# A state space and expert kernel: the front taken by pairs of batches, D as a diagonal matmul, deviations on GpSimd

## The chip, the cores and the metric

One core of a Trainium2 chip. The metric is the device time of one execution in microseconds (us), as the median of several runs. PE is TensorE, DVE VectorE, ACT ScalarE, POOL GpSimd; SP issues most DMAs.

## What is computed

For u of 16 batches x 512 positions x 256 features:

```python
xn = layernorm(u)
Bu = einsum('bld,nd->bln', xn, B_w)              # 64 states
h  = causal convolution over l with sigmoid(log_lambda) ** t, per state
y  = einsum('bln,dn->bld', h, C_w) + D * xn
aff = (xn @ waff.T) / (|xn| * |waff|)            # 8 experts
# best expert of each row, kept if its rank in its batch and expert is below a capacity
# that comes from the mean of all aff and the threshold
out = u + y + sum over experts of (gelu(xn * mask @ W1 + b1) @ W2 + b2)
```

A row that an expert does not get still adds gelu(b1) @ W2 + b2 of that expert (the "zero rows" of the code).

## The kernel before

**Front.** A batch is 512 positions, held as 128 partitions of 4 quarters of 256 features (`QD` = 1024 columns). For each of 16 batches:

- DVE takes `bn_stats` of each quarter (`moments`, L926), aggregates them for two batches (`variance`, L933, L935); ACT takes the root (`deviation`, L519), DVE makes 1/deviation with one Newton step and -mean/deviation (`rstd_of`, L943 to L947).
- ACT normalises the four quarters (`normal`, L525). PE transposes them (`turn`, L675) into `ps_t`, ACT copies that to `xnt` (`turned`, L533), two buffers.
- PE multiplies by 64 columns of B and 8 of waff at once (`states_in`, L693, 72 output rows), DVE runs the recurrence on all 72 rows with one scan instruction (`states`, L953; the factor is 0 for the 8 router rows). PE transposes the 8 rows back (`routed`, L699) and multiplies the states by C (`states_out`, L707) into `ps_y`. DVE adds `ps_y` to the row base (`add_y`, L959).
- POOL makes `D * xn` (L394) and adds it to u (L398), four quarters each; this is the base to which y is added.

Beside this, 12 of the 16 weight units (W1 and W2 of 8 experts) are split into a high and a low f16 part: ACT sums the absolute values (`weight_sum`, L538), PE brings the sum to all partitions (`bound`, L721), DVE makes a power of two of it (`weight_scales`, L963 to L967), ACT makes the high part (`high_part`, L544), DVE the low part (`low_part`, L982). Which batch has which of these steps is written in the tables `SUMS` and `HIGHS`. SP's queue brings in u and the weights and stores xn and base to DRAM. Raw weights lie in a ring of four, and the split parts take the places of xn and base of earlier batches (`home_free`).

**Passage.** From the numerators of all batches (`ps_num`) DVE makes the affinities (L1092) and the best expert; PE transposes them (L761); DVE finds the capacity and the keys (from L1103), counts (L1128 to L1137 behind PE's L780, L781) and places; ACT searches the thresholds (L598 to L600). PE also makes the zero rows (`zero_row`, L750). POOL then gathers the rows of each tile by indirect DMAs.

**Tiles.** 39 tiles of 256 rows go through W1 (L836 to L838), Gelu on ACT, a split on DVE, W2 (L860 to L862), DVE's last operations, and an indirect store. This part is not changed.

Each engine runs its instructions in the order in which they are written; all waits are semaphores written by hand. What a PE instruction waits for also holds all that stands behind it.

## Time and profile before

| | us |
|---|---|
| median of 3 runs | 648.92 (647.56 to 649.32) |
| the profiled execution | 647.61 |
| its span | 645.9 |
| PE busy in the span | 586.8 (91%) |
| DVE busy | 500.3 (77%) |
| POOL busy | 460.1 (71%) |
| ACT busy | 339.8 (53%) |
| mean granted clock of TensorE, share of full speed | 0.951 |

The page of the profile gives busy time per engine, groups of instructions by line, and the chain of work that ended last. Busy time of PE counts overlapping records once. A wait that the trace ascribes to an engine is one that this engine ended last.

### The profile page before, as it was taken

The page shows a single profiled execution, that of the slowest core. Times are in us where ns is not written, and L with a number is a line of the kernel's source. Part 1 is how long each engine was busy: PE and PEld are TensorE (multiplying, and loading weights), DVE is VectorE, ACT ScalarE, POOL GpSimd, SP SyncE. Part 2 cuts the span into 40 slices and gives each one's busy share as a digit, 9 for nine tenths or more (in the row PEclk, how much of TensorE's full clock was granted, in tenths as well). Part 3 has the DMA queues.
Part 4 walks back from the last instruction along what each step waited for, and adds up shares of the span by engine and source line. Part 5 has one row for each costly group of instructions (what it writes and reads, how often), then busy time and mean ns, then how long its engine had stood idle before and what let it go on. Part 6 is the DMA issues. An engine that isn't in the chain of part 4 may idle for free.

```text
span 645.9 us, 15995 instructions
## 1 busy us (share of the span) xinstructions
PE 586.8 (91%) x4597; PEld 496.1 (77%) x4598; DVE 500.3 (77%) x971; ACT 339.8 (53%) x637; POOL 460.1 (71%) x629
## 2 busy tenths in 40 slices
PE   2988878898679989978999999999999999999994
PEld 1655555666567879867898989898998989898983
DVE  5789989798999699669778676767676777767673
ACT  4877859755867926534535353535353444444440
POOL 1999987940068626888788888887778777878463
PEclk9988869897897999989999999999999999999998
DMA  8994776628310214342212222222112112211100
GB/s 312 411 371 150 247 254 186 225 110 261 130 43 17 60 30 155 130 132 59 83 58 81 64 66 81 64 71 73 55 47 70 57 44 73 73 45 29 49 30 2
DMA packets 33587, 72.63 MB, mean 112 GB/s; under 512 B 6519, under 2 KB 19088, under 8 KB 33552
## 3 DMA queue, kind: packets, MB, share of 16 engines
q1 hardware_dynamic: 21488, 46.67, 20.5%
q0 software_dynamic: 11232, 25.20, 12.8%
q10 hardware_dynamic: 832, 0.31, 0.2%
q8 instruction: 19, 0.31, 0.2%
q14 instruction: 16, 0.13, 0.1%
HBM read 50.64 MB, written 27.00 MB: 120 GB/s over the span
## 4 chain that ended last, share of the span: by engine, by line
PE 61%; DVE 19%; issue 8%; ACT 6%; POOL 4%; DMA 1%; DVEq 0%; ACTq 0%; POOLq 0%; SPq 0%
PE ps_bu L860 9%; PE ps_bu L861 9%; PE ps_bu L862 9%; PE ps_t L836 4%; PE ps_t L838 4%; PE ps_t L837 4%; PE ps_y L837 4%; PE ps_y L838 4%; PE ps_y L836 4%; ACT area L525 2%; PE ps_y L707 2%; PE ps_bu L693 2%; PE ps_t L675 2%; POOL out L452 2%; DVE wsum L991 1%
## 5 line engine op out<-in xcount | busy, mean ns | idle before, releaser
L860 PE MATMUL ps_bu<-area,ring 128*128 x624 | 170.1, 273 | 1.9 <-issue 1.8
L861 PE MATMUL ps_bu<-area,ring 128*128 x624 | 170.1, 273 | 0.0
L862 PE MATMUL ps_bu<-area,ring 128*128 x624 | 170.1, 273 | 0.0
L1295 DVE SCALAR_TENSOR_TENSOR ring<-ring,h_scale 128x512 f16<-128x512 f32 x156 | 117.8, 755 | 5.5
L638 ACT ACTIVATE ring<-ps_t,b1t,inv_in 128x256 f32<-128x256 f32 x156 | 79.4, 561 | 56.4 <-PE ps_t L838 46.0
L452 POOL DMA_INDIRECT out<-ring,idx_b x78 | 93.0, 1193 | 18.3 <-issue 13.4
L437 POOL DMA_INDIRECT work<-xn_rows,idx_x x78 | 86.7, 1112 | 26.2 <-issue 21.1
L462 POOL DMA_INDIRECT work<-base_rows,idx_b x78 | 90.9, 1165 | 18.0 <-issue 15.2
L1304 DVE SCALAR_TENSOR_TENSOR ring<-ps_bu,inv_out,work 128x256 f32<-128x256 f32 x78 | 34.1, 479 | 77.5 <-PE ps_bu L862 75.8
L638 ACT ACTIVATE ring<-ps_y,b1t,inv_in 128x256 f32<-128x256 f32 x156 | 79.4, 562 | 21.7 <-PE ps_y L838 21.1
L836 PE MATMUL ps_t<-work,area 128*128 128x256 f16 x312 | 87.0, 279 | 2.4 <-issue 2.2
L838 PE MATMUL ps_t<-work,area 128*128 128x256 f16 x312 | 87.0, 279 | 0.0
L837 PE MATMUL ps_t<-work,area 128*128 128x256 f16 x312 | 87.0, 279 | 0.0
L385 POOL TENSOR_TENSOR small<-ones 128x1 f32<-128x1 f32 x156 | 46.4, 297 | 55.6 <-DVE ring L1319 23.7
L836 PE MATMUL ps_y<-work,area 128*128 128x256 f16 x312 | 85.2, 273 | 0.0
L837 PE MATMUL ps_y<-work,area 128*128 128x256 f16 x312 | 85.2, 273 | 0.0
L838 PE MATMUL ps_y<-work,area 128*128 128x256 f16 x312 | 85.2, 273 | 0.0
L1292 DVE TENSOR_SCALAR ring<-ring,h_scale 128x512 f16<-128x512 f32 x156 | 79.3, 509 | 2.1 <-issue 0.3
L394 POOL TENSOR_TENSOR work<-area,d_bc 128x256 f32<-128x256 f32 x64 | 59.2, 957 | 20.9 <-DMA thr_bc<-L_ffn_affinity_threshold 12.0
L860 PEld LDWEIGHTS ps_bu<-area,ring 128*128 128x128 f16 x624 | 61.0, 98 | 9.4 <-issue 2.4
L861 PEld LDWEIGHTS ps_bu<-area,ring 128*128 128x128 f16 x624 | 61.0, 98 | 7.2
L862 PEld LDWEIGHTS ps_bu<-area,ring 128*128 128x128 f16 x624 | 61.0, 98 | 7.0
(272 smaller groups left out, 1075.4 us busy)
## 6 DMA issues: line engine op xcount, KB each, us to landing
ring<-L_ffn_W SPq DMA_DIRECT2D x14, 1024.0 KB, 6.5
xn_rows<-area SPq DMA_DIRECT2D x8, 1024.0 KB, 8.7
base_rows<-area SPq DMA_DIRECT2D x8, 1024.0 KB, 6.9
area<-L_attn_u SPq DMA_DIRECT2D x7, 1024.0 KB, 18.5
work<-L_ffn_W SPq DMA_DIRECT2D x4, 1024.0 KB, 6.1
area<-L_ffn_W SPq DMA_DIRECT2D x2, 1024.0 KB, 6.3
work<-xn_rows,idx_x POOLq DMA_INDIRECT x78, 2.8
work<-base_rows,idx_b POOLq DMA_INDIRECT x78
```

The source lines that it names most:

```text
L437: g.indirect_dma_start(out=xg[r % 2][:, h * D:(h + 1) * D], out_offset=None, in_=xn_dram, in_offset=bass.IndirectOffsetOnAxis(ap=idx_x[:, ...
L452: g.indirect_dma_start(out=out_rows, out_offset=bass.IndirectOffsetOnAxis(ap=idx_b[:, 2 * ro + h:2 * ro + h + 1], axis=0), in_=og[ro % 2][ ...
L462: g.indirect_dma_start(out=bg[rb % 2][:, h * D:(h + 1) * D], out_offset=None, in_=base_dram, in_offset=bass.IndirectOffsetOnAxis(ap=idx_b[ ...
L638: ins = a.activation(h32[:, c * W:(c + 1) * W], ps_h[qt][:, c % CQ * W:(c % CQ + 1) * W], ACT.Gelu, bias=b1t[:, bass.ds(e * C + c, 1)], sc ...
L836: t.matmul(dst, wh, xhi[p][:, k, :], start=(k == 0), stop=False)
L837: t.matmul(dst, wh, xlo[p][:, k, :], start=False, stop=False)
L838: last = t.matmul(dst, wl, xhi[p][:, k, :], start=False, stop=(k == K - 1))
L860: t.matmul(dst, hh, wh, start=(c == 0), stop=False)
L861: t.matmul(dst, hh, wl, start=False, stop=False)
L862: last = t.matmul(dst, hl, wh, start=False, stop=(c == C - 1))
L1292: v.tensor_scalar(hhi[p][:, cs], h32[:, cs], h_scale[:, bass.ds(e, 1)], None, ALU.mult).then_inc(s["f_hhi"], 1)
L1295: v.scalar_tensor_tensor(out=hlo[p][:, cs], in0=h32[:, cs], scalar=h_scale[:, bass.ds(e, 1)], in1=hhi[p][:, cs], op0=ALU.mult, op1=ALU.sub ...
```

## The change

- Batches are taken by pairs. `states_in` writes the 64 states of the first batch to partitions 0 to 63 and those of the second to 64 to 127; one scan serves both. C and lambda are loaded twice, for both halves.
- `routed` no longer transposes rows of the scan. It multiplies the transposed xn by the 8 columns of waff, 16 matmuls per pair, and needs no scan.
- D * xn is no longer made on POOL. PE multiplies transposed xn by the diagonal of D (two 128x128 blocks) and accumulates onto C's product, in two halves `states_out(i, 0)` and `(i, 1)` per pair; `add_y` comes in two halves too and adds to u itself. `xnt` has four buffers.
- The aggregation, the root and Newton's steps go from DVE and ACT to POOL (`deviations`: 19 operations on 128x8 per pair, with a power of -0.5 and two Newton steps).
- ACT normalises three quarters of a batch, POOL the fourth.
- Sums, bounds, scales, high and low parts come in pairs. The last two of the 12 high parts stand behind the affinities. The places of xn and base in `area` are changed, and so is the order of SP's queue.
- At the end `routed` of the last pair stands ahead of its states; the zero rows 0 and 1 stand behind the transposes of the affinities.

```diff
-        d_bc = sb("d_bc", D)
+        diag = sb("diag", K * P)
+        diag_k = diag[:, :].rearrange("p (k d) -> p k d", k=K)
...
+        xnt = [part(work, at, QD).rearrange("p (k s) -> p k s", k=K) for at in (3 * QD, 4 * QD + E * D + TE, 0, QD)]
...
             def xn_store(i):
                 sp.wait_ge(s["xn_ok"], 2 * i + 2)
+                sp.wait_ge(s["xq_ok"], 2 * i + 2)
...
+            for i in range(1, 5):
+
+                base_store(i)
+                xn_store(i + 3)
+                raw_in(2 * i + 2)
+                raw_in(2 * i + 3)
...
-            pool.wait_ge(s["p_late"], 4 * 16)
-            for b in range(B):
-
...
+            minus_half = cnt[:, 6:7]
+            g.memset(minus_half, -0.5)
+
+            def deviations(i):
+
+                c = slice(2 * i * Q, (2 * i + 2) * Q)
+                st = stats[:, 12 * i * Q:12 * (i + 1) * Q].rearrange("p (t m) -> p t m", m=6)
+                r_, v_, n_, d_, m_ = rstd[:, c], ve[:, c], newt[:, c], sq_d[:, c], sum_d[:, c]
+                pool.wait_ge(s["st_ok"], i + 1)
+                g.tensor_tensor(mean2[:, c], st[:, :, 1], st[:, :, 4], ALU.add)
+                g.tensor_tensor(m_, st[:, :, 2], st[:, :, 5], ALU.add)
+                link(g.tensor_tensor(d_, st[:, :, 1], st[:, :, 4], ALU.subtract))
+                g.tensor_scalar(m_, m_, 1.0 / D, None, ALU.mult)
+                link(g.tensor_tensor(d_, d_, d_, ALU.mult))
+                link(g.tensor_scalar(d_, d_, 0.25, None, ALU.mult))
+                link(g.tensor_tensor(var[:, c], m_, d_, ALU.add))
+                link(g.tensor_scalar(v_, var[:, c], EPS, None, ALU.add))
+                link(g.tensor_tensor(r_, v_, minus_half.to_broadcast([P, 2 * Q]), ALU.pow))
+                for _ in range(2):
+                    link(g.tensor_tensor(n_, r_, r_, ALU.mult))
+                    link(g.tensor_tensor(n_, n_, v_, ALU.mult))
+                    link(g.tensor_scalar(n_, n_, -0.5, 1.5, ALU.mult, ALU.add))
+                    link(g.tensor_tensor(r_, n_, r_, ALU.mult))
+                link(g.tensor_tensor(n_, mean2[:, c], r_, ALU.mult))
+                g.tensor_scalar(nmr[:, c], n_, -0.5, None, ALU.mult).then_inc(s["rstd_ok"], 1)
+                pool.wait_ge(s["rstd_ok"], i + 1)
+
+            for i in range(PAIRS):
+                deviations(i)
+                for b in (2 * i, 2 * i + 1):
+
+                    for q in (3,):
+                        t, cols = b * Q + q, slice(q * D, (q + 1) * D)
+                        last = g.tensor_scalar(xn_(b)[:, cols], xu_(b)[:, cols], rstd[:, t:t + 1], nmr[:, t:t + 1],
+                                               ALU.mult, ALU.add)
+                    last.then_inc(s["xq_ok"], 1)
...
             def normal(b):
                 act.wait_ge(s["rstd_ok"], b // 2 + 1)
-                for q in range(Q):
+                for q in range(3):
...
             def turned(b):
+
+                wait(act, s["y_ok"], b // 2 * 2 - 2)
+                wait(act, s["num_ok"], b // 2 - 1)
                 for k in range(K):
                     act.wait_ge(s["xt_ok"], K * b + k + 1)
-                    wait(act, s["bu_ok"], b - 1)
-                    a.copy(xnt[b % 2][:, k, :], ps_t[:, k * S:(k + 1) * S]).then_inc(s["xt_out"], 1)
+                    a.copy(xnt[b % 4][:, k, :], ps_t[:, k * S:(k + 1) * S]).then_inc(s["xt_out"], 1)
...
-            deviation(0)
             normal(0)
             normal(1)
             turned(0)
-            act.wait_ge(s["p_early"], 4 * 16)
-            a.activation(lam[0:N, 1:2], lam[0:N, 0:1], ACT.Exp, scale=-1.0).then_inc(s["lam_exp"], 1)
-            for b in range(B):
-
-                if b % 2 == 0 and b // 2 + 1 < PAIRS:
-                    deviation(b // 2 + 1)
-                if b + 1 < B:
-                    turned(b + 1)
-                if b + 2 < B:
-                    normal(b + 2)
-                if b == 1:
+            act.wait_ge(s["p_early"], 6 * 16)
+            a.activation(lam[:, 1:2], lam[:, 0:1], ACT.Exp, scale=-1.0).then_inc(s["lam_exp"], 1)
+            turned(1)
+            normal(2)
+            normal(3)
+            for i in range(PAIRS - 1):
+
+                if i + 2 < PAIRS:
+                    normal(2 * i + 4)
+                    normal(2 * i + 5)
+                if i >= 2:
+                    for n in (2 * i - 4, 2 * i - 3):
+                        high_part(n, raw_at(n))
...
+                turned(2 * i + 2)
+                turned(2 * i + 3)
+                if i == 0:
                     act.wait_ge(s["b1_ok"], 1)
                     a.activation(small[:, 0:E], ps_g[:, 0:E], ACT.Sqrt).then_inc(s["act_const"], 1)
                     a.activation(gelu_b[:, :], b1t[:, :], ACT.Gelu).then_inc(s["gelu_ok"], 1)
-                if b == 13:
-                    act.wait_ge(s["xnorm_ok"], 1)
-                    a.activation(sq0, xnorm, ACT.Sqrt).then_inc(s["xroot_ok"], 1)
-                if b in HIGHS:
-                    high_part(HIGHS.index(b), raw_at(HIGHS.index(b)))
-                if b in SUMS:
-                    weight_sum(SUMS.index(b))
+                else:
+                    weight_sum(2 * i - 2)
+                    weight_sum(2 * i - 1)
...
+            for n in (EARLY - 2, EARLY - 1):
+                high_part(n, raw_at(n))
...
-            def states_in(b):
-                pe.wait_ge(s["xt_out"], K * (b + 1))
-                wait(pe, s["scan_ok"], b - 1)
+            turn(1)
+
+            def states_in(i):
+
+                pe.wait_ge(s["xt_out"], K * (2 * i + 2))
+                wait(pe, s["scan_ok"], i - 1)
                 for k in range(K):
-                    last = t.matmul(ps_bu[b % 2][0:NE, :], bwk[:, k, :], xnt[b % 2][:, k, :], start=(k == 0), stop=(k == K - 1))
+                    for h in range(2):
+                        last = t.matmul(ps_bu[i % 2][h * N:(h + 1) * N, :], bwk[:, k, 0:N], xnt[(2 * i + h) % 4][:, k, :],
+                                        start=(k == 0), stop=(k == K - 1))
                 last.then_inc(s["bu_ok"], 1)
 
-            def routed(b):
-                pe.wait_ge(s["scan_ok"], b + 1)
-                for q in range(Q):
-                    last = t.transpose(ps_num[:, q * P + b * E:q * P + (b + 1) * E], every_q(hs[b % 2][N:NE, :], q),
-                                       ident[N:NE, N:NE])
+            def routed(i):
+
+                pe.wait_ge(s["xt_out"], K * (2 * i + 2))
+                for b in (2 * i, 2 * i + 1):
+                    for q in range(Q):
+                        for k in range(K):
+                            last = t.matmul(ps_num[:, q * P + b * E:q * P + (b + 1) * E], every_q(xnt[b % 4][:, k, :], q),
+                                            bwk[:, k, N:NE], start=(k == 0), stop=(k == K - 1))
                 last.then_inc(s["num_ok"], 1)
 
-            def states_out(b):
-                pe.wait_ge(s["scan_ok"], b + 1)
-                wait(pe, s["base_ok"], b)
-                for q in range(Q):
-                    last = t.matmul(ps_y[:, q * D:(q + 1) * D], every_q(hs[b % 2][0:N, :], q), ct[0:N, :],
-                                    start=True, stop=True)
+            def states_out(i, r):
+
+                pe.wait_ge(s["scan_ok"], i + 1)
+                pe.wait_ge(s["diag_ok"], 1)
+                wait(pe, s["base_ok"], 2 * i + r)
+                for n in range(2):
+                    q = 2 * r + n
+                    for h in range(2):
+                        t.matmul(ps_y[:, h * 2 * D + n * D:h * 2 * D + (n + 1) * D], every_q(hs[i % 2][h * N:(h + 1) * N, :], q),
+                                 ct[h * N:(h + 1) * N, :], start=True, stop=False)
+                    for h in range(2):
+                        for k in range(K):
+                            at = h * 2 * D + n * D + k * P
+                            last = t.matmul(ps_y[:, at:at + P], every_q(xnt[(2 * i + h) % 4][:, k, :], q), diag_k[:, k, :],
+                                            start=False, stop=(k == K - 1))
                 last.then_inc(s["y_ok"], 1)
...
-            for b in range(B):
-                if b + 1 < B:
-                    turn(b + 1)
-                states_in(b)
-                if b == 0:
+            for i in range(PAIRS - 1):
+                if i > 0:
+                    states_out(i - 1, 0)
+                states_in(i)
+                if i == 0:
                     constants()
-                if b > 0:
-                    routed(b - 1)
-                    if b < B - 1:
-                        states_out(b - 1)
-                if b - 1 in SUMS:
-                    n = SUMS.index(b - 1)
-                    pe.wait_ge(s["wsum_ok"], n + 1)
+                else:
+                    states_out(i - 1, 1)
+                turn(2 * i + 2)
+                routed(i)
+                turn(2 * i + 3)
+                if i > 0:
+
+                    pe.wait_ge(s["wsum_ok"], 2 * i)
                     pe.wait_ge(s["dve_const"], 2)
-                    wait(pe, s["wscale_ok"], n)
-                    bound(n, ps_g[:, 0:P]).then_inc(s["bound_ok"], 1)
+                    wait(pe, s["wscale_ok"], i - 1)
+                    for n in range(2):
+                        last = bound(2 * i - 2 + n, ps_g[:, n * P:(n + 1) * P])
+                    last.then_inc(s["bound_ok"], 1)
+            routed(PAIRS - 1)
+            states_out(PAIRS - 2, 0)
+            states_in(PAIRS - 1)
+            states_out(PAIRS - 2, 1)
...
-            zero_row(0)
-            zero_row(1)
-            routed(B - 1)
...
-            states_out(B - 2)
+            zero_row(0)
+            states_out(PAIRS - 1, 0)
+            zero_row(1)
             zero_row(2)
...
+            def states(i):
+                dve.wait_ge(s["bu_ok"], i + 1)
+                wait(dve, s["y_ok"], 2 * i - 2)
+                v.tensor_tensor_scan(hs[i % 2], lam_c.to_broadcast([P, S]), ps_bu[i % 2][:, :], 0.0,
                                      ALU.mult, ALU.add).then_inc(s["scan_ok"], 1)
 
-            def add_y(b):
-                dve.wait_ge(s["y_ok"], b + 1)
-                dve.wait_ge(s["dx_ok"], 2 * b + 2)
-                v.tensor_tensor(xu_(b), ps_y[:, :], xu_(b), ALU.add).then_inc(s["base_ok"], 1)
+            def add_y(i, r):
+
+                dve.wait_ge(s["y_ok"], 2 * i + r + 1)
+                for h in range(2):
+                    x = xu_(2 * i + h)[:, r * 2 * D:(r + 1) * 2 * D]
+                    last = v.tensor_tensor(x, ps_y[:, h * 2 * D:(h + 1) * 2 * D], x, ALU.add)
+                last.then_inc(s["base_ok"], 1)
...
+            for i in range(PAIRS - 1):
+                if i > 0:
+                    add_y(i - 1, 0)
+                if i >= 2:
+                    weight_scales(i - 2)
+                states(i)
+                if i > 0:
+                    add_y(i - 1, 1)
+                if i == 0:
+                    setup()
+                if i + 3 < PAIRS:
+                    moments(2 * i + 6)
+                    moments(2 * i + 7)
+                if i == 0:
+                    w_norms()
...
+                if i >= 2:
+                    for n in (2 * i - 4, 2 * i - 3):
+                        low_part(n, raw_at(n))
...
+            add_y(PAIRS - 2, 0)
+            states(PAIRS - 1)
+            add_y(PAIRS - 2, 1)
+            weight_scales(UNIT_PAIRS - 1)
```

Order of PE in a pass of the loop. Before, from one batch to the next (L675 turn, L693 states, L699 router's transposes, L707 output by C, L721 bound):

```order
L675 MATMUL ps_t<-ident,area 128x128 x8
L693 MATMUL ps_bu<-work,bwt 72x512 x2
L699 MATMUL ps_num<-ident,work 128x8 x4
L707 MATMUL ps_y<-ct,work 128x256 x4
L721 MATMUL ps_g<-ident,wsum 128x128
L675 MATMUL ps_t<-ident,area 128x128 x8
L693 MATMUL ps_bu<-work,bwt 72x512 x2
L699 MATMUL ps_num<-ident,work 128x8 x4
L707 MATMUL ps_y<-ct,work 128x256 x4
```

With the change, one pass, from the second half of states_out(i-1, 0) on (L742 is C, L747 is D, L720 states, L699 turn, L730 the router's numerators, L761 the two bounds):

```order
L742 MATMUL ps_y<-ct,work 128x256 x2
L747 MATMUL ps_y<-diag,work 128x128 x4
L720 MATMUL ps_bu<-work,bwt 64x512 x4
L742 MATMUL ps_y<-ct,work 128x256 x2
L747 MATMUL ps_y<-diag,work 128x128 x4
L742 MATMUL ps_y<-ct,work 128x256 x2
L747 MATMUL ps_y<-diag,work 128x128 x4
L699 MATMUL ps_t<-ident,area 128x128 x8
L730 MATMUL ps_num<-bwt,work 128x8 x16
L699 MATMUL ps_t<-ident,area 128x128 x8
L761 MATMUL ps_g<-ident,wsum 128x128 x2
```

The bound stood behind the states and the output of the next batch; the two bounds now stand directly behind the second turn of the pass.

Order of ACT in the same place, before (L538 weight sum, L519 root, L533 copies of the turned batch, L525 normal, L544 high part):

```order
L538 ACTIVATE work,wsum<-ring 128x2048
L519 ACTIVATE rstd<-work 128x8
L533 COPY work<-ps_t 128x512 x2
L525 ACTIVATE area<-area,work,rstd 128x256 x4
L544 ACTIVATE area<-ring,scale_w 128x2048
L538 ACTIVATE work,wsum<-ring 128x2048
```

With the change, one pass and the start of the next (L541 normal, L562 high parts, L551 copies, L556 weight sums):

```order
L541 ACTIVATE area<-area,work,rstd 128x256 x6
L562 ACTIVATE area<-ring,scale_w 128x2048 x2
L551 COPY work<-ps_t 128x512 x4
L556 ACTIVATE work,wsum<-ring 128x2048 x2
L541 ACTIVATE area<-area,work,rstd 128x256 x6
```

The sums for which the two bounds wait are made behind the copies of both batches that PE turned last before those bounds.

Order of PE at the end of the front, before (L750 zero rows, L761 transposes of the affinities, L780 and L781 the counts):

```order
L699 MATMUL ps_num<-ident,work 128x8 x4
L721 MATMUL ps_g<-ident,wsum 128x128
L750 MATMUL ps_t<-ring,gelu_b 128x256 x16
L699 MATMUL ps_num<-ident,work 128x8 x4
L761 MATMUL ps_t<-ident,work 128x128 x4
L764 MATMUL ps_num<-small,ones 128x1
L707 MATMUL ps_y<-ct,work 128x256 x4
L750 MATMUL ps_g<-ring,gelu_b 128x256 x8
L780 MATMUL ps_bu<-rc,tri 128x8
L781 MATMUL ps_bu<-rc,ones 128x8
```

With the change, from the end of states_out(6, 1) to the counts (L806 transposes of the affinities, L798 zero rows, L827 and L828 the counts):

```order
L747 MATMUL ps_y<-diag,work 128x128 x4
L806 MATMUL ps_t<-ident,work 128x128 x4
L809 MATMUL ps_num<-small,ones 128x1
L798 MATMUL ps_t<-ring,gelu_b 128x256 x8
L742 MATMUL ps_y<-ct,work 128x256 x2
L747 MATMUL ps_y<-diag,work 128x128 x4
L742 MATMUL ps_y<-ct,work 128x256 x2
L747 MATMUL ps_y<-diag,work 128x128 x4
L798 MATMUL ps_t<-ring,gelu_b 128x256 x8
L798 MATMUL ps_g<-ring,gelu_b 128x256 x8
L827 MATMUL ps_bu<-rc,tri 128x8
L828 MATMUL ps_bu<-rc,ones 128x8
```

Zero rows 0 and 1 moved from ahead of the transposes of the affinities to behind them, and one more half output stands between these and the counts; ahead of these rows the last pair's states and both halves of the output of pair 6 come after the last numerators.

## Rows read from the trace of the kernel before

**Rows 1.** stretches: us, busy us (instructions) of each engine, PEclk, DMA share, GB/s

```profile
80.00:100.00 20.00, 16.66 (x51) 11.02 (x52) 17.97 (x39) 12.78 (x19) 17.82 (x21) 0.66 0.59 208
300.00:400.00 100.00, 100.00 (x919) 90.04 (x917) 76.27 (x138) 42.12 (x81) 81.91 (x123) 1.00 0.23 71
```

**Rows 2.** chain of waits, in order of time: start us, us, what

```profile
128.21 1.71 PE ps_t L675 x8
```

**Rows 3.** groups by line, first 170 us: count | busy us, mean ns | idle us before

```profile
L394 POOL TENSOR_TENSOR work<-area,d_bc 128x256 f32<-128x256 f32 x64 | 59.2, 957 | 20.9 <-DMA thr_bc<-L_ffn_affinity_threshold 12.0 <-ACT area L525 7.5
...
L707 PE MATMUL ps_y<-ct,work 64*128 64x256 f32 x128 | 41.1, 469 | 10.8 <-DVE area L959 10.8
...
L982 DVE SCALAR_TENSOR_TENSOR area<-ring,scale_w,area 128x2048 f16<-128x2048 f32 x10 | 24.6, 2461 | 0.1
...
L959 DVE TENSOR_TENSOR area<-ps_y,area 128x1024 f32<-128x1024 f32 x16 | 19.5, 1216 | 0.1
L953 DVE TENSOR_TENSOR_SCAN work<-lam,ps_bu 72x512 f32<-72x512 f32 x16 | 19.2, 1203 | 0.1
```

**Rows 4.** timeline of DVE: a small operation by itself and beside POOL's products

```profile
8.97 0.17 DVE L945 TENSOR_TENSOR work<-work 128x8 f32<-128x8 f32 x1
...
31.56 0.65 DVE L945 TENSOR_TENSOR work<-work 128x8 f32<-128x8 f32 x1
```

**Rows 5.** timeline: a small operation of POOL, the slow cast of DVE

```profile
2.19 0.22 POOL L371 CAST iota_f<-ring 128x40 f32<-128x40 int32 x1
...
178.23 2.14 DVE L1198 CAST tile_expert<-work 128x39 int32<-128x39 f32 x1
```

**Rows 6.** ACT: two copies (timeline), and a weight sum (chain of waits)

```profile
22.80 1.07 ACT L533 COPY work<-ps_t 128x512 f32<-128x512 f32 x2 [0.74 <-PE ps_t L675]
...
78.02 1.99 ACT work L538 x2
```

**Rows 7.** timeline of PE, 67 to 78 us

```profile
67.41 1.97 PE L675 MATMUL ps_t<-ident,area 128*128 128x128 f32 x8 [1.15 <-ACT area L525]
...
72.34 2.24 PE L707 MATMUL ps_y<-ct,work 64*128 64x256 f32 x8
74.51 0.49 PE L721 MATMUL ps_g<-ident,wsum 128*128 128x128 f32 x2
74.83 1.04 PE L675 MATMUL ps_t<-ident,area 128*128 128x128 f32 x8
75.71 1.88 PE L693 MATMUL ps_bu<-work,bwt 128*72 128x512 f32 x4
77.52 0.64 PE L699 MATMUL ps_num<-ident,work 8*128 8x8 f32 x4
```

**Rows 8.** timeline of PE's weight loads: three series of short passes

```profile
21.29 0.52 PEld L716 LDWEIGHTS ps_g<-ring,ones 128*128 128x128 f32 x4
...
169.04 0.63 PEld L773 LDWEIGHTS ps_num<-area 128*128 128x128 f16 x16 [4.79 <-DVE area L1186]
...
202.65 0.97 PEld L721 LDWEIGHTS ps_bu<-ident,wsum 128*128 128x128 f32 x8
```

**Rows 9.** timeline of the start, DVE, ACT and PE

```profile
4.42 2.88 DVE L926 BATCH_NORM_STATS2 work<-area 128x6 f32<-128x256 f32 x8 [4.29 <-DMA area<-L_attn_u]
...
9.57 4.04 ACT L525 ACTIVATE area<-area,work,rstd 128x256 f32<-128x256 f32 x8 [1.15 <-DVE work L947]
...
11.79 1.94 PE L675 MATMUL ps_t<-ident,area 128*128 128x128 f32 x8 [11.79 <-ACT area L525]
```

**Rows 10.** timeline of the end of the front

```profile
146.93 0.69 DVE L1092 TENSOR_TENSOR work<-ps_num,work 128x512 f32<-128x512 f32 x1 [0.73 <-PE ps_num L699]
...
150.55 0.69 DVE L1103 TENSOR_SCALAR_CACHE_REDUCE work<-work 128x512 f32<-128x512 f32 x1
...
159.36 0.16 DVE L1137 COPY end<-ps_bu 128x8 f32<-128x8 f32 x1
...
160.93 3.32 PEld L750 LDWEIGHTS ps_g<-ring,gelu_b 128*128 128x128 f32 x16 [0.23 <-issue]
```

More of the change, by code:

```diff
@@ L1016, in _ @@
             dve.wait_ge(s["consts"], 1)
-            link(v.tensor_scalar(lam[0:N, 2:3], lam[0:N, 1:2], 1.0, None, ALU.add))
-            link(v.reciprocal(lam[0:N, 3:4], lam[0:N, 2:3]))
+            link(v.tensor_scalar(lam[:, 2:3], lam[:, 1:2], 1.0, None, ALU.add))
+            link(v.reciprocal(lam[:, 3:4], lam[:, 2:3]))
+            moments(4)
+            moments(5)
             def setup():
@@ L1022, in setup @@
                 v.tensor_copy(c_bc[:, :], ps_g[:, 128:128 + D])
+                v.tensor_copy(d_col, ps_g[:, 384 + E * C:384 + E * C + K])
                 v.tensor_copy(b1t[:, :], ps_g[:, 384:384 + E * C]).then_inc(s["b1_ok"], 1)
+                dve.wait_ge(s["b1_ok"], 1)
+                for k in range(K):
+                    last = v.tensor_scalar(diag_k[:, k, :], ident[:], d_col[:, k:k + 1], None, ALU.mult)
+                last.then_inc(s["diag_ok"], 1)
                 dve.wait_ge(s["b1_ok"], 1)
@@ L1226, in kept @@
                 link(v.tensor_tensor(thr, bits[:, 3:4].bitcast(F32), sign, ALU.mult))
-                gt, run = gap, pick
+                gt = gap_kept
                 link(v.tensor_scalar(gt, a_rows, thr, 0.0, ALU.is_gt, ALU.add, accum_out=cnt[:, 3:4]))
```

215 lines of the change are left out of this document (73 added, 142 removed).

## Prediction

> **What bounds the kernel now.** I read, in this order, the table of stretches, the chain of waits, the groups by line of the first 170 us and the timelines of a few batches. The stretches [rows 1] divide the span in two: from 300 us on PE is busy without a break (100.00 of 100 us) at a granted clock of 1.00, while from 80 to 100 us no engine is quite full and the clock is 0.66. The change touches only the front (16 batches) and the passage from it to the expert tiles. A microsecond won or lost there moves everything behind it, since the tiles wait for the row indices that come out of it and then run on PE without slack. In these 20 us of the front DVE is busy 18.0, POOL 17.8, PE 16.7 and ACT 12.8 [rows 1]. The turns of batch 0 begin on PE at 11.79 [rows 9], those of batch 15 at 128.21 [rows 2]: 116.4 us for 15 batches, **15.5 us for a pair**. PE waits 10.8 us for DVE's add L959 before L707 alone [rows 3]. So DVE sets the pace now, with POOL close to it.
>
> **What DVE, ACT and POOL gain.** Per pair DVE loses eight L933, the addition L935 and the five small operations L943 to L947. One of these takes 0.17 us by itself and 0.65 beside POOL's long products [rows 4]; with the wait for ACT's root this is 2 to 5 us. One scan for two batches saves 1.2 us [rows 3]. What stays is 2.9 (statistics [rows 9]), 1.2 (scan), 2.4 (adds), two L982 of 2.46 [rows 3] and some 1 us of scales (five operations of 0.15 to 0.3): **12.4 us per pair**. POOL loses its 16 long operations (0.96 each for L394 [rows 3]) and gets two like them and 19 small ones. A small one takes 0.22 us with 0.06 to the next [rows 5], so 19 x 0.28 = 5.3 us, **7 us per pair** with the two quarters at 0.85. No row shows a power on POOL: 0.2 us is the floor, and the ceiling is 2.1, what a tiny cast took on DVE [rows 5]; I take 0.3, since POOL's other tiny operations lie there. ACT: six L525 of 0.5 (four of them per batch before [rows 9]), two high parts of 2.0, four copies of 0.53 and two sums of 2.0 [rows 6]: **13.1 us**. All three are below the 15.5 of now. By these engines alone the change would win.
>
> **What PE pays.** A matmul in f32 leaves two records, a transpose one: L716 is two matmuls, and x4 [rows 8]. I count passes (records) and take the distances between starts, not durations, which overlap. At full clock, per pair:
> - turns: 16 passes, as before. L675 begins at 74.83, the next line at 75.71 [rows 7]: 0.9 a batch, 1.8 a pair.
> - states: 8 passes of 512 columns, as before; 1.81 us per 4 (75.71 to 77.52 [rows 7]), 3.6 in line. They now alternate between two halves of the array's columns.
> - output by C: 16 passes; 2.17 us per 8 (72.34 to 74.51 [rows 7]), 4.3 in line. They now alternate between two halves of its rows.
> - new, D by the diagonal: 16 matmuls, 32 passes of 128 columns. Eight loads of that shape, L721, take 0.97 us, the last one 0.19 [rows 8]: a distance of 0.11. 32 x 0.11 = **3.5**.
> - new, the router's numerators by matmuls, in place of eight transposes of 1.1 us: 32 passes of 8 columns. L716 has exactly that shape: four loads in 0.52 us, the last 0.19 [rows 8], so 0.11 again although only 8 columns follow. **3.5**.
> - bounds: 4 passes, 0.5.
>
> The trace never has work in two halves side by side, so states and C are bounded by the line (3.6 and 4.3) and by half of it (1.8 and 2.15). I take the middle, 2.7 and 3.2: the two passes of one matmul use the same half, so only passes of neighbours can run together. The Trainium skill (TensorEngine Tiling (Array Packing), Key Properties) says that different tiles can execute weight loads and matmuls in parallel, and that a change of tiling mode drains the engine. By the first alone the pair would be 2.0 us shorter than I take it; no row of before shows either. The sum is 1.8 + 2.7 + 3.2 + 3.5 + 3.5 = **14.7 us** without bounds, against 1.8 + 3.6 + 4.3 + 1.1 = 10.8.
>
> **A new wait on PE.** The orders ahead of this text show it. In before a bound stands behind states and output of later batches, and ACT's sum is long done. Now two bounds stand right behind turn(2i+3), and ACT makes the two sums only after it has copied what that turn gives. PE's queue stops for the end of the copies (0.7 us: the second of two in 1.07 [rows 6]), 2 x 1.99 for the sums, and 0.1 for semaphores: **4.8 us** in every pass of the loop, i = 1 to 6. Queued behind it stand output, states and the next turns, and ACT's next copies and sums wait for these. It is a closed circle: turn, copies, sums, bounds, output, states, output, turn, numerators, turn. DVE (12.4) and ACT (13.1) fit inside.
>
> After idle time the granted clock falls from the level of 2.4 to that of 1.2 GHz: a turn costs 1.97 us after a gap of 1.15, and 1.04 otherwise [rows 7]. From 80 to 100 us the mean is 0.66 [rows 1], so 13.6 of 20 us are at the lower level, behind two gaps, 6.8 each. One gap per pass thus costs nothing at best (the low stretch falls in the gap) and 3.4 us at worst (all of it in work); I take the middle, 1.7. A pass is then 14.7 + 4.8 + 0.5 + 1.7 = **21.7 us**, against 15.5.
>
> **The start.** The first statistics end at 7.3 [rows 9]; POOL's deviations end at 12.6, 3 us behind the start of L525 now (9.57), and those of the next pairs at 19.6 and 26.6. ACT takes batches 4 and 5 ahead of the copies of batch 2: 26.6 + 3.1 = 29.7, copy 0.6, then PE's turn(3), 0.9. Pass i = 1 starts at some 31.5. A power of 2.1 us would come in three times, 5.4 us later.
>
> **The end of the front.** 31.5 + 6 x 21.7 = 161.7, numerators 3.5: the affinities start at 165.2, before at 146.93 [rows 10]: **+18.3**. Then PE has 3.35 + 2.7 + 3.35 = 9.4 us of output and states ahead of the transposes of the affinities, and DVE adds and scales until 11.8 us behind the affinities, where L1103 came at 3.6 [rows 10]. Next PE has 1.0 (transposes, sum), zero row 0 (3.4: sixteen L750 [rows 10]), an output (3.35) and zero rows 1 and 2 (6.8) before the counts: 9.4 + 1.0 + 3.4 + 3.35 + 6.8 + 0.4 = 24.4, against 159.36 - 146.93 = 12.4 [rows 10]: **+12.0**. Zero rows 0 and 1 ran beside DVE's long reciprocal before and lose that cover. The two high parts that move behind (4 us of ACT) are covered by DVE's way to the first key; once that is gone they would cost up to 4. From the counts on only the time is shifted. Sum: +18.3 + 12.0 = **+30.3**. The profiled execution took 647.6 us around a span of 645.9; the median is 648.9, 1.3 above it. 647.6 + 30.3 + 1.3 = **679 us**.
>
> **Rivals.**
> 1. *The halves never overlap.* 2.0 us more per pass, 12 over six, 3 at the end: 694 us. For it: in all rows passes are in line. 0.13.
> 2. *Full overlap, and the gap costs no clock.* 2.0 + 1.7 less per pass, 22 us, 3 at the end: 654 us. Against it stand the turns of 1.97 us [rows 7]. The Trainium skill (TensorEngine Tiling (Array Packing), Key Properties) would have the overlap so, but for the drain. 0.09.
> 3. *Faster: loads hide.* If a pass of D and of the numerators costs what one of L773 in f16 does, 16 loads of the same size in 0.63 us [rows 8], (0.63 - 0.10)/15 = 0.035, then 480 passes on the path cost 0.075 less each, 36 us: 643 us. It wins below about 0.045. Against it are L716 and L721, both f32. 0.07.
> 4. *POOL becomes the bound*, with a power or small operations three times as long as its rows: 22 us a pair and a late start, 700 us or more. 0.04.
>
> **How the numbers follow.** My case has the other 0.67. It takes in the clock's bounds (10 us either way) and most of the overlap's, 661 to 696. To leave out no more than 2 in 10 the range is **657 to 697**. About 0.3% (2 us) is what a measurement of this kernel tells from no change. Faster: rival 3, 0.07. Within it: the lower edge of rival 2, 0.03. Slower: 0.90.
>
> **What would show it.** PE idle 4 to 5 us before six pairs of bounds, released by the sums on ACT; passes 20 to 23 us apart; DVE busy some 12 us per pass; D and numerators at distances of 0.11; affinities at 165, counts 24 behind them; the tiles as before. Passes of C from the two halves with the same start would show overlap. I am wrong if PE has no gap before the bounds, or if a pass takes under 17 us.

## The result, and the profile after

The changed kernel takes **743.86 us** (742.8 to 744.35, 4 runs) against 649.12 in the same series, a ratio of 1.146 (1.1434 to 1.1486). The forecast was 679 us with a range up to 697: the sign was right, the size was not. Single runs of a kernel are now and then slower; the ratios, here and below, leave those out, the medians do not. The profiled execution took 741.1 us of span, 95.2 more than before.

The stretches of the changed kernel (us, busy us and instructions of each engine, PEclk, DMA share, GB/s) answer to [rows 1]:

```profile
80.00:100.00 20.00, 15.33 (x66) 13.31 (x64) 8.10 (x12) 9.21 (x14) 10.56 (x21) 0.57 0.56 210
...
400.00:500.00 100.00, 100.00 (x917) 90.03 (x916) 73.02 (x133) 42.58 (x83) 81.79 (x122) 1.00 0.24 73
```

The tiles run as before. In the front DVE fell from 18.0 to 8.1 us of 20, POOL from 17.8 to 10.6, ACT from 12.8 to 9.2. Part of that is only that a pair now takes almost twice as long. Counted over one whole pass for a pair (94.35 to 124.31) DVE was busy 11.9 us, ACT 13.1 and POOL 10.6, where the forecast had 12.4, 13.1 and 7; in the kernel before, from 30 to 123 us, it was 13.9, 11.8 and 13.9 in 15.5. So DVE and POOL were relieved, ACT was not, and none of the three fills a pass; yet the front takes 75 us longer. Two rows on DVE date that, the use of the router's numerators and the copy of the counts:

```profile
222.54 0.69 DVE L1121 TENSOR_TENSOR work<-ps_num,work 128x512 f32<-128x512 f32 x1 [11.42 <-PE ps_num L730]
...
252.96 0.17 DVE L1172 COPY end<-ps_bu 128x8 f32<-128x8 f32 x1 [4.87 <-PE ps_bu L828]
```

Against [rows 10] the affinities are 75.6 us late and the counts 93.6. The timeline of PE shows a whole pass of the loop, from one pair of bounds (L761) to the next (L742 C, L747 D, L720 states, L699 turn, L730 numerators):

```profile
94.35 1.23 PE L761 MATMUL ps_g<-ident,wsum 128*128 128x128 f32 x4 [4.67 <-ACT work L556]
...
95.50 1.25 PE L742 MATMUL ps_y<-ct,work 64*128 64x256 f32 x4
...
96.68 2.23 PE L747 MATMUL ps_y<-diag,work 128*128 128x128 f32 x8
...
101.99 1.94 PE L720 MATMUL ps_bu<-work,bwt 128*64 128x512 f32 x8
...
103.86 0.84 PE L742 MATMUL ps_y<-ct,work 64*128 64x256 f32 x4
...
104.63 2.13 PE L747 MATMUL ps_y<-diag,work 128*128 128x128 f32 x8
...
109.44 1.04 PE L699 MATMUL ps_t<-ident,area 128*128 128x128 f32 x8
...
110.31 7.53 PE L730 MATMUL ps_num<-bwt,work 128*128 128x8 f32 x32
...
117.69 1.95 PE L699 MATMUL ps_t<-ident,area 128*128 128x128 f32 x8
...
124.31 1.22 PE L761 MATMUL ps_g<-ident,wsum 128*128 128x128 f32 x4 [4.67 <-ACT work L556]
```

Taken from start to start, as the prediction did, this pass of 29.96 us stands beside the forecast of 21.7:

| part of a pass, us | forecast | measured | from |
|---|---|---|---|
| two turns | 1.8 | 1.7 | 109.44 to 110.31, twice |
| states, 8 passes | 2.7 | 1.9 | 101.99 to 103.86 |
| C, 16 passes | 3.2 | 3.1 | 103.86 to 104.63, four times |
| **D, 32 passes** | 3.5 | **8.2** | 104.63 to 106.69, four times |
| **numerators, 32 passes** | 3.5 | **7.4** | 110.31 to 117.69 |
| gap ahead of the bounds | 4.8 | 4.7 | its row |
| bounds | 0.5 | 0.5 | taken as forecast |
| lower clock | 1.7 | 2.5 | what is left of 29.96 |

Two rows are wrong by more than a factor of two, together 8.6 us of a pass. The groups by line of the first 230 us say it in another way, by the mean of a weight load (mean ns after the comma):

```profile
L730 PEld LDWEIGHTS ps_num<-bwt,work 128*128 128x128 f32 x256 | 60.4, 329 | 0.0
...
L747 PEld LDWEIGHTS ps_y<-diag,work 128*128 128x128 f32 x208 | 50.5, 327 | 9.9 <-issue 9.9
...
L699 PEld LDWEIGHTS ps_t<-ident,area 128*128 128x128 f32 x128 | 22.7, 204 | 15.5 <-issue 15.5
```

A load of a turn takes 204 ns on average, one of D or of the numerators 327 to 329, of the same 128x128 in f32. (These are durations; they overlap, so the distance between two starts is shorter.) What differs is how the stationary operand lies in SBUF: a turn takes 128 neighbouring words, `every_q` takes every fourth, a step of 16 bytes. That gave the theory for the runs: **the strided read of the weights costs 0.235 us a pass.** ("Weights" are here the stationary operand of any matmul.) Its rivals were that the eight columns behind a load, the clock, or a switch between halves of the array cost it; and beside that, how much of the loss is the gap of 4.67 us instead.

### The profile page after: what moved, and what is told of

Read it like the earlier page. It is cut to its first block, busy times and chain, and to the rows that moved or that the text cites. A ratio compares the mean times of both kernels' runs of the same rounds, so it can differ in the third digit from the quotient of the medians.

```text
span 741.1 us, 16704 instructions
## 1 busy us (share of the span) xinstructions
PE 670.0 (90%) x5045; PEld 586.4 (79%) x5046; DVE 463.8 (63%) x840; ACT 332.1 (45%) x612; POOL 412.7 (56%) x670
## 4 chain that ended last, share of the span: by engine, by line
PE 77%; DVE 6%; ACT 5%; issue 5%; POOL 4%; DMA 2%; DVEq 0%; ACTq 0%; POOLq 0%; SPq 0%
PE ps_y L747 8%; PE ps_num L730 8%; PE ps_bu L907 7%; PE ps_bu L909 7%; PE ps_bu L908 7%; PE ps_t L883 4%; PE ps_t L885 4%; PE ps_t L884 4%; PE ps_y L885 4%; PE ps_y L883 4%; PE ps_y L884 4%; PE ps_y L742 4%; PE ps_t L699 3%; ACT work L556 3%; PE ps_bu L720 2%
## 5 line engine op out<-in xcount | busy, mean ns | idle before, releaser
L457 POOL DMA_INDIRECT work<-xn_rows,idx_x x78 | 85.0, 1090 | 26.6 <-issue 21.3
L482 POOL DMA_INDIRECT work<-base_rows,idx_b x78 | 88.8, 1139 | 18.0 <-issue 15.2
L883 PE MATMUL ps_t<-work,area 128*128 128x256 f16 x312 | 85.8, 275 | 3.8 <-issue 3.7
L988 DVE TENSOR_TENSOR area<-ps_y,area 128x512 f32<-128x512 f32 x32 | 20.6, 686 | 108.7 <-PE ps_y L747 108.6
L884 PE MATMUL ps_t<-work,area 128*128 128x256 f16 x312 | 85.7, 275 | 0.0
L885 PE MATMUL ps_t<-work,area 128*128 128x256 f16 x312 | 85.6, 274 | 0.0
L382 POOL TENSOR_TENSOR small<-ones 128x1 f32<-128x1 f32 x156 | 49.9, 320 | 61.4 <-DVE ring L1354 23.7
L747 PEld LDWEIGHTS ps_y<-diag,work 128*128 128x128 f32 x256 | 62.2, 327 | 11.2 <-issue 11.2
L747 PE MATMUL ps_y<-diag,work 128*128 128x128 f32 x256 | 68.7, 419 | 0.0
L907 PEld LDWEIGHTS ps_bu<-area,ring 128*128 128x128 f16 x624 | 61.1, 98 | 8.3 <-issue 1.2
```

The lines of the kernel that those rows point to most:

```text
L457: g.indirect_dma_start(out=xg[r % 2][:, h * D:(h + 1) * D], out_offset=None, in_=xn_dram, in_offset=bass.IndirectOffsetOnAxis(ap=idx_x[:, ...
L482: g.indirect_dma_start(out=bg[rb % 2][:, h * D:(h + 1) * D], out_offset=None, in_=base_dram, in_offset=bass.IndirectOffsetOnAxis(ap=idx_b[ ...
L747: last = t.matmul(ps_y[:, at:at + P], every_q(xnt[(2 * i + h) % 4][:, k, :], q), diag_k[:, k, :], start=False, stop=(k == K - 1))
L883: t.matmul(dst, wh, xhi[p][:, k, :], start=(k == 0), stop=False)
L884: t.matmul(dst, wh, xlo[p][:, k, :], start=False, stop=False)
L885: last = t.matmul(dst, wl, xhi[p][:, k, :], start=False, stop=(k == K - 1))
```

## The experiments

**Loads by themselves.** A kernel that computes nothing of the reference (it copies u to the output) and has PE do series of matmuls, each on a line of its own; the stationary tile's step, rows and type and the columns behind vary. A first form, e1_loads, had all series in one helper line, so the profile joined them and no series could be read from it. The second gives each its own line:

```diff
+ for _ in range(24):
+     t.matmul(ps0[:, 0:8], at(w, 1), x[:, 0:8], **once)
+ for _ in range(24):
+     t.matmul(ps0[:, 0:8], at(w, 4), x[:, 0:8], **once)
...
+ for n in range(16):
+     t.matmul((ps0, ps1)[n % 2][:, 0:256], at(w, 4, 0, n % 2 * 64, 64), x[n % 2 * 64:n % 2 * 64 + 64, 0:256], **once)
```

> The same series as in the first load kernel, each on a code line of its own, so that each can be read. Theory S: 0.11 us per f32 pass at stride 1 and about 0.235 at stride 4 with 128 rows, with 8 or 128 columns behind it, the same at the lower clock (last two series), since in the changed kernel a D pass took 0.24 us in stretches of either clock. If it is the clock of PE that drives the load, the stride 4 series at the lower clock takes 0.47. With 64 rows 0.235, with 8 rows 0.11. Rival R: 0.11 in all series. Halves: 0.21 to 0.27 us per pass in one half, 0.11 to 0.14 in alternating halves.

The timeline of the weight loads (L48, L50, L52, L54: step 1, 2, 4, 8 with 8 columns behind; L56, L58: step 4 with 64 and 8 rows; L60, L62: step 1 and 4 with 128 columns; L64, L66: f16, step 1 and 4; L68: step 1 in one half of the rows, L70 and L72: step 1 and 4 in halves by turns, 256 columns):

```profile
20.26 7.05 PEld L48 LDWEIGHTS ps<-x,w 128*128 128x128 f32 x48
27.19 10.36 PEld L50 LDWEIGHTS ps<-x,w 128*128 128x128 f32 x48
37.43 11.30 PEld L52 LDWEIGHTS ps<-x,w 128*128 128x128 f32 x48
48.63 11.51 PEld L54 LDWEIGHTS ps<-x,w 128*128 128x128 f32 x48
60.16 11.27 PEld L56 LDWEIGHTS ps<-x,w 64*128 64x128 f32 x48
71.46 11.27 PEld L58 LDWEIGHTS ps<-x,w 8*128 8x128 f32 x48
82.75 8.38 PEld L60 LDWEIGHTS ps<-x,w 128*128 128x128 f32 x48
91.05 11.28 PEld L62 LDWEIGHTS ps<-x,w 128*128 128x128 f32 x48
102.13 1.48 PEld L64 LDWEIGHTS ps<-x,w 128*128 128x128 f16 x48
103.54 1.68 PEld L66 LDWEIGHTS ps<-x,w 128*128 128x128 f16 x48
105.23 12.56 PEld L68 LDWEIGHTS ps<-x,w 64*128 64x128 f32 x32
117.46 4.74 PEld L70 LDWEIGHTS ps<-x,w 64*128 64x128 f32 x32
122.02 4.02 PEld L72 LDWEIGHTS ps<-x,w 64*128 64x128 f32 x32
```

Two stretches of it, those of L52 and of L62 (columns as above, with DVE and POOL alone of the others):

```profile
37.50:48.70 11.20, 11.20 (x50) 11.20 (x50) 0.00 (x0) 0.00 (x0) 0.50 0.01 1
...
91.00:102.20 11.20, 11.20 (x51) 11.20 (x51) 0.00 (x0) 0.00 (x0) 1.00 0.00 0
```

From start to start, a load of step 4 takes 11.20/48 = 0.233 us at a clock of 0.50 with 8 columns behind (L52), and 11.08/48 = 0.231 at 1.00 with 128 columns (L62). 64 rows or 8 make it no cheaper (0.235). Step 2 costs 10.24/48 = 0.213 at 0.50. The contiguous one follows the clock and not the columns: with 8 columns its loads start 0.112 apart at a clock of 1.00 (L48, 21 to 23 us), with 128 columns 0.112 at 1.00 and 0.213 at 0.50 (L60, 89 to 91 and 84 to 85 us). In f16 the step matters little, 0.029 against 0.035. No series up to L66 changes halves, and nothing else runs beside them. So columns, rows, clock, halves and other engines are ruled out, and the step in f32 is what costs. The changed kernel says the same: in the numerators from 110.31 on the clock falls from 1.00 to 0.50 at some 113.5 us, and the loads start 0.231 apart before it and 0.233 behind it. The durations alone could not have told: a contiguous load lasts 333 ns at 0.50 (L60) and 192 at 1.00. Halves by turns with step 4 take 4.02/32 = 0.126 a pass: two strided loads run side by side. That fits C, whose stationary tile is strided as well and which was not made worse.

The Trainium skill (Advanced Engine Details and Errata, SBUF Cachelines) says that SBUF is read in lines of 16 bytes, that two hits on a line are needed to hide its latency, and that another line for each access costs. The runs agree: one word of a line (f32, step 4 and 8) costs 0.233 and 0.240, two words of a line (f32, step 2; f16, step 4) little or nothing. Step 2 was only seen at 0.50, so whether it is free at full clock stays open.

**The weights contiguous.** In e2_contiguous a turn writes its result quarter by quarter, so that D and the numerators read neighbouring words; the matmuls of the states put their output in the old order instead.

```diff
- last = t.transpose(every_q(ps_t[:, k * S:(k + 1) * S], q),
+ last = t.transpose(ps_t[:, k * S + q * P:k * S + (q + 1) * P],
...
- ... every_q(xnt[b % 4][:, k, :], q), ...
+ ... xnt[b % 4][:, k, q * P:(q + 1) * P], ...
```

> The turned batch is written quarter by quarter, so that the stationary operands of D and of the numerators are contiguous; the states' matmuls write their output in the order of positions. Same number of instructions. Theory S: D and numerators fall from 0.235 us to 0.11 us per pass, 64 passes or 8 us in each of six passes of the loop, and some 110 passes at start and end: 744 - 62 = 682 us, with the gap of 4.7 us before the bounds unchanged. Rival R (full rows, or contention in SBUF): no change, 744. A third possibility: the states' matmuls get slower by their strided output, up to 2 us per pass of the loop, 690 to 695.

Measured: 697.42 us (696.62 to 701.66), ratio 1.0772 (1.0717 to 1.0828): **46.4 us less**, where 62 were expected. The weight loads of one of its passes:

```profile
103.47 0.93 PEld L762 LDWEIGHTS ps_g<-ident,wsum 128*128 128x128 f32 x4 [5.07 <-ACT work L556]
...
105.80 1.78 PEld L748 LDWEIGHTS ps_y<-diag,work 128*128 128x128 f32 x8 [0.63 <-issue]
...
113.30 0.97 PEld L748 LDWEIGHTS ps_y<-diag,work 128*128 128x128 f32 x8 [0.23 <-issue]
...
116.92 3.69 PEld L731 LDWEIGHTS ps_num<-bwt,work 128*128 128x128 f32 x32
120.41 1.70 PEld L699 LDWEIGHTS ps_t<-ident,area 128*128 128x128 f32 x8
```

The numerators now take 3.49 us for 32 (116.92 to 120.41), 0.109 each: the forecast's own figure. But eight loads of D take 0.97 at full clock and 1.78 directly behind the gap: a contiguous load follows the clock, a strided one didn't. So more hangs on the low clock here than in the changed kernel, and the pass is 23.3 us on average, not the 21.7 of the forecast's sum; it fell by 6.5 us and not by the 8 expected. The states are no slower by their strided output (110.66 to 112.53, 1.87 us), so the third possibility is out.

**The gap away.** e3_sums_early changes only ACT's order: the two weight sums stand ahead of the high parts and the copies.

```diff
  for i in range(PAIRS - 1):
      normal(2 * i + 4); normal(2 * i + 5)
+     weight_sum(2 * i - 2); weight_sum(2 * i - 1)
...
-     weight_sum(2 * i - 2); weight_sum(2 * i - 1)
```

> The changed kernel with ACT's two weight sums ahead of the high parts and the copies, nothing else. Theory G (closed circle through the sums): PE's idle time before the bounds, 58 us over two records of 6 x 4.7, disappears; 6 x 5 = 29 us, and up to 1.7 us per pass more from the clock: 705 to 715 us. Rival: ACT is then late with the copies, because it waits for the weights or for the scales, and the gap comes back in front of the numerators: 735 to 745.

Measured: 712.18 us (709.97 to 713.72), ratio 1.0977 (1.0928 to 1.1026), **31.7 us less**. PE runs through, with no wait ahead of the bounds:

```profile
101.55 7.53 PE L730 MATMUL ps_num<-bwt,work 128*128 128x8 f32 x32
108.93 1.95 PE L699 MATMUL ps_t<-ident,area 128*128 128x128 f32 x8
110.67 1.06 PE L761 MATMUL ps_g<-ident,wsum 128*128 128x128 f32 x4
```

The pass fell from 29.8 to 24.3 us: 4.7 of gap and 0.8 of clock. The numerators stay at 7.4. The low clock did not go away with the gap: in this run too it falls from 1.00 to 0.50 at some 105 us, inside the numerators, while PE is busy without a break, and the turn behind them takes 1.95 us where the other takes 1.04.

**Both.** e4_both has the two edits together.

> Both edits together. If both terms are as stated and independent: 744 - 62 - 29 = 653 us, with the clock's part 643 to 653. If they are not independent, because ACT (13 us per pass) or DVE becomes the next bound once PE needs only 15 us: 660 to 670.

Measured: 668.82 us (668.15 to 670.12), ratio 1.031 (1.027 to 1.035). It saves 75.0 us of 94.7, where the two alone saved 78.1: they are two causes, nearly additive. The 653 us for independent terms was too low mainly because the 62 in it was: with the savings as measured it would be 665.7. The time lies in the second range, 660 to 670, and a next bound does show. Its timeline of PE shows one pass without a wait, and where one is left:

```profile
92.88 1.94 PE L699 MATMUL ps_t<-ident,area 128*128 128x128 f32 x8 [5.43 <-ACT work L551]
94.61 1.06 PE L762 MATMUL ps_g<-ident,wsum 128*128 128x128 f32 x4
...
110.60 1.06 PE L762 MATMUL ps_g<-ident,wsum 128*128 128x128 f32 x4
```

16.0 us for this pass (94.61 to 110.60), 18.7 on average: now POOL and ACT show. The waits of its first 160 us (in total, times, longest):

```profile
ACT area L541 <- POOL work L408: 31.7, 7, 8.8
...
PE ps_t L699 <- ACT work L551: 10.2, 3, 5.4
```

**Do the halves overlap?** e6_half_order issues the states half by half instead of by turns, in the changed kernel.

```diff
- for k in range(K):
-     for h in range(2):
+ for h in range(2):
+     for k in range(K):
```

> The changed kernel with the four matmuls of the states in the order first half twice, second half twice, where they alternated. Theory O (only neighbours in different halves run side by side, in order): one pair of neighbours is left, so 7 of 8 passes are in line and a group takes 3.0 to 3.3 us instead of 1.87; eight groups, 9 to 11 us more in all, 753 to 755. Rival (no overlap at all; 64 columns are simply cheaper than 72): 1.87 us and 744 as before. Other rival (the engine looks far enough ahead): 1.87 and 744 too, told from the first by the starts of single passes.

Its one run took 742.07 us, and the states as long as before:

```profile
102.26 1.94 PE L720 MATMUL ps_bu<-work,bwt 128*64 128x512 f32 x8
104.13 0.84 PE L742 MATMUL ps_y<-ct,work 64*128 64x256 f32 x4
```

Eight passes of 512 columns in 1.87 us is what four took in [rows 7] (1.81): the overlap is complete, in either order. The first rival, that a pass of 64 columns is cheaper than one of 72, is out: in both runs the passes start by twos, 0.43 us from one two to the next, and from the second two on each lasts 592 ns, which is also the median of L693 in the kernel before. Which two passes run together is left open: the two of a pair start 6 to 7 ns apart with the halves by turns and 14 with half by half, which does not say whether they belong to one matmul or to both halves. In C four passes of 256 columns take 0.77, against 1.09 in line [rows 7]: part of the overlap.

**What is left.** e7_stats_early takes e4 and has DVE make the statistics one pass earlier, since ACT waited for POOL's deviations (31.7 us above) and POOL for these.

```diff
- if i + 3 < PAIRS:
-     moments(2 * i + 6); moments(2 * i + 7)
+ if i + 4 < PAIRS:
+     moments(2 * i + 8); moments(2 * i + 9)
```

> The version with contiguous operands and early sums, and in addition the statistics of a pair one pass of the loop earlier on DVE, so that POOL's deviations, for which ACT waited 25 us between 25 and 145 us, are there in time. Theory: the 10 us that PE waits for ACT's copies in that version go away, 669 - 10 = 659 us. Rival: ACT waits for the weights in place of that (it did so twice, 5.4 us), 663 to 669.

Measured: 662.25 us (660.52 to 663.88), ratio 1.021 (1.0184 to 1.0237), between the two expectations. ACT's wait for POOL fell from 31.7 to 11.5 us in the first 150, but it now waited 14.7 us for the weights, in six places, and PE's wait for the copies went down from 10.2 to 5.3 us only: the rival came true in part. Affinities at 145.3, before the 146.93 of [rows 10]: the front alone is level with before. The counts are 25.3 behind them, though, twice the 12.4 of before. e8_tail_order therefore also puts the last pair's states and outputs and the zero rows behind what leads to the counts, and orders DVE's part in the same way.

```diff
  states_out(PAIRS - 2, 0)
- states_in(PAIRS - 1); states_out(PAIRS - 2, 1)
  ... transposes of the affinities ...
- zero_row(0); states_out(PAIRS - 1, 0); zero_row(1); zero_row(2)
+ states_in(PAIRS - 1); states_out(PAIRS - 2, 1)
  ... counts ...
+ states_out(PAIRS - 1, 0); zero_row(0); states_out(PAIRS - 1, 1); zero_row(1); zero_row(2)
```

> In addition the end of the front is ordered by what waits: the transposes of the affinities and the counts come ahead of the last states, outputs and of all zero rows, DVE does the keys and the counts ahead of the last adds; one transposed batch lies in another place, so that this is free of races. Theory: the counts come 13 to 16 us behind the affinities where they came 25.4 behind, 10 to 12 us less than the version before it: 647 to 649, about the kernel before (648.5). Rival: the zero rows, now all between counts and tiles on PE, are late for the first tiles and give back half: 653 to 655.

Measured: 658.47 us (653.05 to 661.56), ratio 1.0143 (1.0103 to 1.0184). The counts came 16.1 behind the affinities (157.6), 9 us sooner, but the tiles started only at 196.3 (before 188.86): the zero rows stand late, as in the second expectation, and the median is above even its 653 to 655. e9_zero_row moved one of them ahead of the counts, where PE was idle for 3.2 us.

```diff
+ zero_row(0)
  ... counts ...
  states_out(PAIRS - 1, 0)
- zero_row(0)
```

> The version with all four edits, with zero row 0 moved ahead of the counts. In the run before it TensorE was idle 3.2 us there, and VectorE was idle 5.2 us behind the zero row that stood between the two outputs of the last pair. If the passage from the counts to the tiles is set by TensorE's own queue, the counts stay within 1 us (157 to 158), the second add of the last pair comes some 3.5 us sooner (166), the first transposes of the first tile stand at 192.5 to 193.5 instead of 196.3, and the median falls by 3 to 4 us, to 654 to 656, still slower than before. If instead the row indices or the gathered rows set it, the tiles start where they did and the median stays within 1 us of 658.5.

Measured: 655.82 us (652.94 to 661.64), ratio 1.013 (1.0088 to 1.0171), which can't be told from the run before it (1.0103 to 1.0184). The median lies where the first expectation had it, but not for its reason: the idle time had only moved. PE now waited 3.9 us between the two outputs of the last pair, for DVE's add behind the key's rank, and the tiles started at 195.58 and not at 192.5 to 193.5. e10_two_rows puts zero row 1 there.

```diff
  states_out(PAIRS - 1, 0)
+ zero_row(1)
  states_out(PAIRS - 1, 1)
- zero_row(1)
```

> As the run before, with zero row 1 now between the two outputs of the last pair, where TensorE was idle 3.9 us. If TensorE's own queue sets the passage, the 3.9 us go: the first transposes of the first tile come at 192 instead of 195.6, and the median falls by some 3 us, to 652 to 654. If the row indices set it (they were ready at 187.7, and the gathered rows are needed behind them), the tiles start less than 1 us sooner and the median stays at 655 to 657.

In this series the kernel before took 658.87 us, 10 more than in the others, so only the ratio is read: 662.76 us (657.35 to 672.51), **1.0036 (1.0002 to 1.0071)**. Its timeline of PE:

```profile
164.56 3.62 PE L801 MATMUL ps_t<-ring,gelu_b 128*128 128x256 f32 x16
168.65 0.84 PE L747 MATMUL ps_y<-ct,work 64*128 64x256 f32 x4 [0.47 <-DVE area L993]
...
197.00 0.60 PE L872 MATMUL ps_num<-ident,work 128*128 128x128 f32 x4
```

From the counts (161.49) to the tiles it takes 35.5 us, where e9 took 38.9 (156.69 to 195.58): 3.4 of the 3.9 us of wait are gone, and PE's own queue sets this passage, as the first expectation had it. Its times (192, 652 to 654) can't be read in a slower series; the ratio fell by 0.009, some 6 us, where 3 were expected, and what the rest is stays open. That is as near to the kernel before as a version came; none beat it. PE still carries, per pair, 64 passes of D and numerators (7.0 us at 0.109) in place of eight transposes of 1.1 us.

## Why the prediction was wrong

**The step that failed** is the price of a pass of D and of the numerators: "a distance of 0.11. 32 x 0.11 = 3.5", twice. It was taken from L721 and L716 [rows 8], of the same size and type, but without a step over words: L716 reads neighbouring words, L721 one word again and again (`to_broadcast`). The change reads every fourth word, and that costs 0.235. Over six passes the two terms are 6 x 8.6 = 51.6 us. The strided load stood in the trace of before, in the groups by line of its first 170 us:

```profile
L707 PEld LDWEIGHTS ps_y<-ct,work 64*128 64x128 f32 x128 | 32.9, 324 | 13.0 <-issue 11.2
L675 PEld LDWEIGHTS ps_t<-ident,area 128*128 128x128 f32 x128 | 20.0, 183 | 21.0 <-issue 11.7 <-ACT area L525 8.2 <-DVE ring L1014 1.1
```

L707's stationary tile is strided, and its loads took 324 ns on average, against 183 for those of L675. Its matmuls stand in [rows 3] and [rows 7], and I read from them only how long 256 columns take. Rows of the same shape are not rows of the same access. The Trainium skill's rule on lines of 16 bytes, above, spoke against this change and was not weighed.

What the sum misses otherwise, from 30.3 to the measured 95.2 us of span:
- *Start*, 36.38 instead of 31.5, +4.9. Two causes lie side by side. On PE the numerators of pair 0 take 3.9 us more and stand ahead of turn(3), which follows them without a wait. And the power on POOL (L401) takes 1.67 us, not 0.3, three times in a row: nearer to the ceiling of 2.1 than to the value taken. With shorter numerators, in e2, turn(3) waits for ACT until 33.42 and the loop starts at 35.29, only 1.1 us sooner. So POOL's cause by itself leaves 3.8 of the 4.9, and PE's by its rows would bring 3.9.
- *Six passes*, (214.98 - 36.38)/6 = 29.8 instead of 21.7: +48.4, by the table above.
- *Last numerators*, 214.98 to the affinities at 222.54, 7.6 instead of 3.5: +4.1.
- *From the affinities to the counts*, 30.4 instead of 24.4: +6.0. Three half outputs cost 5.6 to 6.2 instead of 3.35 (+7.3), the zero rows 0.3 more, the states 1.9 instead of 2.7, the transposes of the affinities 0.6 instead of 1.0.
- These make 63.3 of the 64.9 missing (93.6 at the counts, less 30.3); 1.6 came behind the counts.

**What was right.** The place and the size of the new wait: 4.67 us ahead of each of the six pairs of bounds, released by the weight sum of ACT, forecast 4.8; e3 removes it and gets back 31.7 us, 5.3 per pass. That DVE, ACT and POOL have room, though POOL was priced too low: 10.6 us in the pass above instead of 7. That the tiles don't change. The end of the front as a queue of PE's own. The states overlap fully, 0.8 us better than the middle that I took; C is at the middle. Rival 1 (no overlap) is refuted. That much of rival 2 came true, but not its gap that costs no clock. Rival 3 (loads of 0.035) is refuted in the other direction. Rival 4 (POOL as the bound) had its premise in part: a power of 1.7 us in every pair and, in this pass, two small operations of 2.2 and 2.3 beside DVE's L1012,

```profile
113.63 2.23 POOL L393 TENSOR_TENSOR work<-work 128x8 f32<-128x8 f32 x1 [18.03 <-DVE work L973]
...
115.82 2.30 POOL L394 TENSOR_TENSOR work<-work 128x8 f32<-128x8 f32 x1
...
119.80 1.67 POOL L401 TENSOR_TENSOR rstd<-work,small 128x8 f32<-128x8 f32 x1
```

but POOL had waited 18 us for the statistics ahead of them, so it was not the bound.

**Near by luck.** The clock's term, 1.7 us forecast and 2.5 measured, was put down to the gap. The gap is not what brings the low level: the granted clock fell to 0.50 at some 113.5 us, inside the numerators, with PE busy, 6 us ahead of the gap, and the turn at 117.69 already took 1.95. In e3, without a gap, the clock fell at the same place of the pass; with the gap the low clock cost 0.8 us more. What makes the clock fall there stays open.

The range was too narrow for one reason: it had bounds for overlap and clock, and none for the load, which was the largest term and rested on two rows that seemed exact.

## What to carry to other kernels

Before the price of a matmul is taken from a row, compare the operands' access, not only their shape: the stationary tile in f32 should be contiguous, or be laid out so by whoever writes it, which here cost nothing (the states, with their output in another order, take 1.87 us as in the changed kernel) and gave 46 us. When work is moved to an engine's in-order queue, look at what it will wait for there and put that first on the engine that makes it; moving the queued work out of the way of what others wait for gave most of the rest here (31.7 us for two lines of ACT's order), but no order won anything over the kernel in which PE didn't have that work.

## What the hardware showed beyond expectation

- A strided f32 load takes 0.231 to 0.240 us at either clock level; a contiguous one 0.109 to 0.112 at the level of 2.4 GHz and 0.21 at that of 1.2. At the low level the step therefore costs a tenth, at the high one it doubles the load.
- A busy PE is not always at full clock. In the series of loads PE and its loads were busy without a break from 27 to 88 us, and the granted clock was 0.50 all the time; it rose to 1.00 inside L60, still with no idle time. In the changed kernel it fell from 1.00 to 0.50 inside the numerators, again without idle time. They took the same 7.4 us, since their loads were strided.
- Two halves of the rows by turns overlap fully. At a granted clock of 1.00 a pass of 256 columns f32 with contiguous weights starts 0.215 us behind the one before it in one half (L68, 105.6 to 106.0 us) and 0.108 by turns (L70, 120.5 to 122.0 us). With a step of 4 it is 0.126 by turns (L72).
